# Expert blocks of one kernel listed by size class, each class in a loop of its own

## The chip, the cores and the metric

The kernel runs on one core of a Trainium2 chip. Times are device microseconds. The metric is the median of the runs of one program. A profile is one further execution of it; its times count from the start of its span.

## What is computed

A transformer layer: cross-attention on a context of 8 x 1601 keys, a self-attention block that adds zeros (its value width is 0), and a mixture of experts with the top 2 of 8 experts for each of 512 tokens. Only the last part is touched:

```python
logits = jnp.einsum('bsd,de->bse', x, router_w) + router_b
top_vals, top_idx = jax.lax.top_k(logits, top_k)
...
h = jax.nn.relu(jnp.einsum('td,edh->eth', xf, w1) + b1[:, None, :])
y = jnp.einsum('eth,ehd->etd', h, w2) + b2[:, None, :]
out = jnp.einsum('etd,te->td', y, gf)
```

x has 512 columns, the hidden layer 2048, all values are float32. Only a token's two chosen experts have a gate above zero.

## The kernel before

The program is one block of five instruction streams (TensorE, VectorE, ScalarE, GpSimd, SyncE) that wait for each other by semaphores. After attention come layer norm, router and gates, and from then on the expert stage.

**Blocks.** The tokens of an expert are worked on in blocks of up to BLOCK = 160 rows: a first part of P = 128 and a second of REST = 32. A block whose expert has at most 128 tokens left is narrow, the others are wide. VectorE works out a table from the tokens per expert (`count_sb`): for each block its expert (`table`), the first rank that it takes (`base`), and whether it is narrow (`narrow`). At the table's end stands the number of blocks. Blocks are listed in the order of the experts. Each step of this calculation waits for the one before it (`step`).

**A block.** Every float32 product is made of rounded high and low parts. For a block each of the 16 chunks c of the hidden layer goes this way: TensorE multiplies the gathered rows `xg_mix` with a piece of w1 (`hidden`, four pairs of products of 2n and n columns, where n is 128 or 160); ScalarE takes one half with the bias out of PSUM (`low_term`, writes `h_part`); VectorE adds the other (`sum_hidden`, writes `h_sum`); ScalarE applies relu and rounds (`relu_high`, writes `h_mix`); VectorE forms the low part (`relu_low`); TensorE multiplies with w2 (`outputs` in a wide block, `outputs_by_rows` with 128 rows as stationary side in a narrow one). Between these, ScalarE rounds a piece of the weights, 128x1024 (`weight_high`, `w_hi`), and VectorE forms its low part (`weight_low`, `w_lo`). TensorE runs two chunks ahead of the outputs: the products of chunks 0 and 1 of block b + 1 come at the end of block b, with 160 columns always. ScalarE's two activations on a chunk have 160 columns always, VectorE's operations have n.

**A block's end.** VectorE copies the next block's bias (`take_bias`, writes `b1_cur`; rows of the profile print `b_cur`), for which ScalarE's next `low_term` waits. In a wide block it then adds the halves of y (`sum_outputs`, writes `yt`) and TensorE turns it (`turn_outputs`); a narrow block has neither. ScalarE multiplies with the gates (`gate_rows`, writes `y_gated`), and GpSimd adds the rows to the output in memory with an indirect transfer.

**The next block's rows** are found on the way: VectorE compares ranks with `base` (`select`), TensorE turns the match into row numbers (`find_rows`), VectorE takes them (`take_rows`), GpSimd gathers the rows, TensorE turns them (`turn_rows`).

**Ahead of the loop** VectorE runs the table, copies the bias, writes the low part of `xg_mix` for block 0 (`gathered_low`) and the low part of a piece of w2, and takes the row numbers. Block 0 always belongs to expert 0, its rows are picked with a product on TensorE. TensorE makes the first two hidden products behind `xg_mix`, then runs `find_rows(0)`.

**The loops.** TensorE and VectorE have one loop over all blocks with an If in it: the code of a narrow block, then that of a wide one. ScalarE, SyncE and GpSimd have one loop and no If. SyncE loads weights two groups of four chunks ahead, whole for each block. The number of blocks and the table's entries are read from SBUF into registers (TENSOR_LOAD in the order of instructions).

```python
with pe.Fori(0, blocks) as b:
    is_narrow = pe.value_load(narrow[0:1, bass.ds(b, 1)], min_val=0, max_val=1)
    with pe.If(is_narrow > 0):
        block(b, P)
    with pe.Else():
        block(b, BLOCK)
```

## Time and profile before

| | us |
|---|---|
| median of 3 runs (1126.29 to 1127.34) | 1126.48 |
| the profiled execution | 1122.11 |
| its span | 1120.4 |
| TensorE busy in it | 1072.0 (96%) |
| VectorE busy | 976.2 (87%) |
| ScalarE busy | 732.2 (65%) |
| GpSimd busy | 504.2 (45%) |

The span runs from the first to the last instruction on the core; the profiled execution's own time has 1.7 us around it. Busy time of TensorE is that of its matmuls, which overlap, so it says that TensorE had work and not that it ran at its peak. PEclk is the granted clock of TensorE as a share of full speed (2.4 GHz; its lower level, 1.2 GHz, is 0.5). Idle time before an instruction stands in brackets with what ended it; "issue" means that the engine waited for nothing that the profile shows.

### The profile page before, as it was taken

The numbers are of one execution on the slowest core, as the hardware profiler recorded it, in microseconds if no ns is written. First come the engines' busy times: TensorE is split into PE (matmuls) and PEld (weight loads), VectorE is DVE, ScalarE is ACT, GpSimd is POOL, SyncE is SP. The second block draws the span as 40 slices with busy tenths as digits, with TensorE's granted clock in tenths as the row PEclk, the third lists the DMA queues.
The fourth block names the chain that finished last, engine by engine and source line by source line (L and its number), as shares of the span: only waits on it lengthen the run. The fifth ranks groups of instructions, "written<-read, shape, count | busy, mean of one in ns | idle before, by whom it ended". The sixth has DMA issues, their size and how long they took to land.

```text
span 1120.4 us, 24041 instructions
## 1 busy us (share of the span) xinstructions
PE 1072.0 (96%) x7583; PEld 1026.6 (92%) x7584; DVE 976.2 (87%) x2242; ACT 732.2 (65%) x1515; POOL 504.2 (45%) x448
## 2 busy tenths in 40 slices
PE   5999999999999999999999999998889999899996
PEld 5899999999999999999999999986778998789886
DVE  7589999989989999999999998988888888888985
ACT  3756665666666656666666565755578777787875
POOL 6564756566647565656475656271021121221211
PEclk9999999999999999999999999999899999999999
DMA  5322121222121212112212121044698877889883
GB/s 195 111 71 69 44 82 42 67 60 63 46 77 48 65 52 71 46 50 73 67 42 81 42 67 51 2 163 151 182 292 275 257 243 238 280 279 282 252 256 112
DMA packets 86369, 138.49 MB, mean 124 GB/s; under 512 B 15816, under 2 KB 40520, under 8 KB 86336
## 3 DMA queue, kind: packets, MB, share of 16 engines
q1 hardware_dynamic: 82800, 130.07, 36.5%
q0 software_dynamic: 3536, 8.00, 3.6%
q8 instruction: 19, 0.31, 0.1%
q14 instruction: 14, 0.11, 0.0%
HBM read 130.88 MB, written 7.17 MB: 123 GB/s over the span
## 4 chain that ended last, share of the span: by engine, by line
PE 75%; DVE 9%; ACT 8%; issue 6%; DVEq 1%; DMA 0%; POOL 0%; ACTq 0%; SPq 0%; POOLq 0%
PE ps L433 13%; PE ps L435 13%; PE ps L434 13%; PE ps L1504 8%; PE ps L1662 8%; PE ps L1554 8%; PE ps L1535 4%; PE ps L1536 4%; PE ps L1663 3%; ACT w_hi L879 2%; ACT w_hi L871 2%; DVE h_mix L1337 1%; ACT h_part L922 1%; DVE h_sum L1331 1%; DVE w_lo L1219 1%
## 5 line engine op out<-in xcount | busy, mean ns | idle before, releaser
L587 POOL TENSOR_TENSOR ctx_hi<-ctx_raw,no_query 128x1152 fp32r<-128x1152 f32 x64 | 142.2, 2221 | 259.8 <-PE ps L435 250.1
L821 ACT ACTIVATE probs<-ps,negmax 128x1152 f32<-128x1152 f32 x64 | 78.4, 1225 | 185.0 <-DVE negmax L1150 185.0
L1051 DVE SCALAR_TENSOR_TENSOR k_mix<-ps,bk_sb,k_mix 64x384 fp32r<-64x384 f32 (+1 forms) x256 | 162.3, 634 | 37.7 <-ACT k_mix L774 32.7
L433 PE MATMUL ps<-wv_hi,ctx_hi 128*128 128x256 f32 (+1 forms) x624 | 180.7, 290 | 2.2 <-DVE k_mix L1051 2.1
L591 POOL TENSOR_TENSOR ctx_lo<-ctx_raw,ctx_hi 128x1152 fp32r<-128x1152 f32 x64 | 179.8, 2809 | 5.0
L435 PE MATMUL ps<-wv_hi,ctx_lo 128*128 128x256 f32 (+1 forms) x624 | 175.0, 280 | 0.0
L434 PE MATMUL ps<-wv_lo,ctx_hi 128*128 128x256 f32 (+1 forms) x624 | 174.6, 280 | 0.0
L1662 PE MATMUL ps<-xg_mix,w_hi 128*128 128x320 f32 (+1 forms) x584 | 157.6, 342 | 14.6 <-DVE h_sum L1331 11.2
L774 ACT ACTIVATE k_mix<-ps,bk_sb 64x384 fp32r<-64x384 f32 (+1 forms) x256 | 150.9, 589 | 21.0 <-PE ps L435 16.7
L1663 PE MATMUL ps<-xg_mix,w_lo 128*128 128x160 f32 (+1 forms) x584 | 135.4, 232 | 0.0
L433 PE MATMUL ps<-ctx_hi,wk_hi 128*128 128x384 f32 (+1 forms) x384 | 133.1, 347 | 0.0
L1173 DVE TENSOR_TENSOR pt_mix<-ps,pt_mix 128x384 fp32r<-128x384 f32 (+1 forms) x256 | 132.9, 581 | 0.1
L1662 PEld LDWEIGHTS ps<-xg_mix,w_hi 128*128 128x128 f32 x584 | 112.5, 193 | 21.8 <-DVE h_sum L1331 14.9
L435 PE MATMUL ps<-ctx_hi,wk_lo 128*128 128x384 f32 (+1 forms) x384 | 132.4, 345 | 0.0
L434 PE MATMUL ps<-ctx_lo,wk_hi 128*128 128x384 f32 (+1 forms) x384 | 131.8, 343 | 0.0
L1147 DVE TENSOR_REDUCE mx<-ps 128x1 f32<-128x384 f32 (+1 forms) x256 | 128.6, 564 | 0.2 <-PE ps L1536 0.2
L779 ACT CAST v_mix<-ps 128x256 fp32r<-128x256 f32 (+1 forms) x208 | 77.4, 373 | 71.0 <-PE ps L435 69.2
L433 PEld LDWEIGHTS ps<-wv_hi,ctx_hi 128*128 128x128 f32 (+1 forms) x624 | 115.1, 184 | 4.3 <-DVE k_mix L1051 3.7
L1663 PEld LDWEIGHTS ps<-xg_mix,w_lo 128*128 128x128 f32 x584 | 114.1, 195 | 2.8
L434 PEld LDWEIGHTS ps<-wv_lo,ctx_hi 128*128 128x128 f32 (+1 forms) x624 | 115.3, 185 | 0.3
L435 PEld LDWEIGHTS ps<-wv_hi,ctx_lo 128*128 128x128 f32 (+1 forms) x624 | 114.9, 184 | 0.0
L832 ACT CAST pt_mix<-ps 128x384 fp32r<-128x384 f32 (+1 forms) x256 | 111.5, 530 | 0.2 <-PE ps L1554 0.2
(236 smaller groups left out, 2606.4 us busy)
## 6 DMA issues: line engine op xcount, KB each, us to landing
w_raw<-in_w_dram SPq DMA_DIRECT2D x76, 1024.0 KB, 6.9
ctx_raw<-in_ctx_t_dram SPq DMA_DIRECT2D x48, 576.0 KB, 3.8
ctx_raw<-in_ctx_t_dram SPq DMA_DIRECT2D x16, 673.5 KB, 4.1
out_dram<-acc POOLq DMA_DIRECT2D x2, 1024.0 KB, 10.2
q_both<-q_scratch SPq DMA_DIRECT2D x14, 128.0 KB, 2.9
x<-in_x_dram SPq DMA_DIRECT2D x4, 256.0 KB, 3.6
wq_raw<-in_wq_dram SPq DMA_DIRECT2D x1, 1024.0 KB, 6.8
q_scratch<-q_out SPq DMA_DIRECT2D x1, 1024.0 KB, 7.0
```

The costliest lines, as they stand in the source:

```text
L433: pe.matmul(acc_ap, a_hi, b_hi, start=start, stop=False)
L434: pe.matmul(acc_ap, a_hi, b_lo, start=False, stop=False)
L435: return pe.matmul(acc_ap, a_lo, b_hi, start=False, stop=stop)
L587: nc.gpsimd.tensor_tensor(ctx_hi[slot][:, :, 0:n], ctx_raw[slot][:, :, 0:n], no_query[:].rearrange("p (o i) -> p o i", o=1).broadcast_to([ ...
L591: nc.gpsimd.tensor_tensor(ctx_lo[slot][:, :, 0:n], ctx_raw[slot][:, :, 0:n], ctx_hi[slot][:, :, 0:n].bitcast(F32), ALU.subtract).then_inc( ...
L774: last = nc.scalar.activation(k_mix[rows, 2 * a + i, KEY0[c]:KEY0[c] + m], ps[rows, bank, 0:m], ACT.Identity, bias=bk_sb[rows, a:a + 1])
L832: nc.scalar.copy(pt_mix[:, TILE0[c]:TILE0[c] + n, 0, :], ps[:, SCORE_BANK + c, 0:n * P].rearrange("p (t r) -> p t r", t=n)).then_inc(pt_hi ...
L1051: last = nc.vector.scalar_tensor_tensor(out=k_mix[other, 2 * a + i, cols], in0=ps[rows, bank, 0:m], scalar=bk_sb[rows, a:a + 1], in1=k_mix ...
L1147: part = nc.vector.tensor_reduce(mx[:, c:c + 1], ps[:, SCORE_BANK + c, 0:KEYS[c]], AX.X, ALU.max)
L1173: nc.vector.tensor_tensor(pt_mix[:, TILE0[c]:TILE0[c] + m, 1, :], ps[:, SCORE_BANK + c, 0:m * P].rearrange("p (t r) -> p t r", t=m), pt_mi ...
L1662: pe.matmul(both, hi, mix[:, :, 0:n], start=first, stop=False)
L1663: return pe.matmul(high, lo, mix[:, 0, 0:n], start=False, stop=end)
```

## The change

The blocks are put in order of size: first block 0, which is expert 0's first 160 tokens and counts as wide whatever expert 0 holds, then the other wide blocks, then the narrow ones. `count_sb` of expert 0 is lowered by 160 for the list. A key of 16 times the size class plus the block's number is compared with all keys (`past`, now 16x16), which gives each block its place, and from it `table` and `base` in the new order. The table ends in three numbers (where the wide ones end, where a class of larger blocks would end, which this size doesn't have, and the number of blocks), and each engine reads all three. The table of flags, `narrow`, is gone. TensorE, VectorE and ScalarE have a loop over wide blocks and, if there are narrow ones, a second loop over these. In narrow blocks ScalarE's two activations have 128 columns, and so have the products of the next block's chunks 0 and 1, if this one is narrow. SyncE and GpSimd keep their one loop. GpSimd fills two more small constants, next to those that it filled before. `yt`, `past` and `past_n` move to other places in SBUF. The calculation of the table on VectorE stands as rows behind the diff.

```diff
     BLOCK = P + REST
+    WIDE = P + P // 4
...
-    MAX_BLOCKS = (TOP_K * T + (E - 1) * (BLOCK - 1)) // BLOCK + 1
+    MAX_BLOCKS = (TOP_K * T + E * (BLOCK - 1)) // BLOCK + 1
     TABLE = MAX_BLOCKS + 1
+    GROUP = 16
+    ENDS = 3
+    assert 2 * BLOCK <= 480 and TABLE <= GROUP
...
+        def ends_loaded(engine):
+
+            return [engine.value_load(table[0:1, TABLE + i:TABLE + i + 1], min_val=1, max_val=MAX_BLOCKS)
+                    for i in range(ENDS)]
...
-            act.wait_ge(table_ready, 1)
-            blocks = act.value_load(table[0:1, TABLE:TABLE + 1], min_val=1, max_val=MAX_BLOCKS)
-            def low_term(b, c):
+            def low_term(b, c, n):
...
-                nc.scalar.activation(h_part[:, c % 2, :], ps[:, hidden_bank(c), BLOCK:2 * BLOCK], ACT.Identity,
+                nc.scalar.activation(h_part[:, c % 2, 0:n], ps[:, hidden_bank(c), BLOCK:BLOCK + n], ACT.Identity,
                                      bias=b1_cur[:, 0, c:c + 1]).then_inc(h_parted, 1)
...
                 take_bias_product(2 * c + 1)
-                relu_high(0, c)
-            with act.Fori(0, blocks) as b:
+            def block_high(b, n, ahead):
...
                 for c in range(HIDDEN_AHEAD, HT):
-                    low_term(b, c)
+                    low_term(b, c, n)
...
+            act.wait_ge(table_ready, 1)
+            wide_end, large_end, blocks = ends_loaded(act)
+            with act.Fori(0, wide_end) as b:
+                block_high(b, WIDE, BLOCK)
+            with act.If(blocks > wide_end):
+                with act.Fori(wide_end, blocks) as b:
+                    block_high(b, P, P)
...
-            select(0, rank_e[:, 0:1, :], 0.0, gates_e[:, 0, :, :])
+            select(0, rank_e[:, 0:1, :], 0.0, gates_e[:, 0, :, :], most=float(WIDE))
...
+            step(nc.vector.tensor_scalar(count_sb[:, 0:1], count_sb[:, 0:1], float(WIDE), 0.0, ALU.subtract, ALU.max))
             step(nc.vector.tensor_scalar(some[:], count, 0.0, None, ALU.is_gt))
-            step(nc.vector.memset(some[:, 0:1], 1.0))
...
+            step(nc.vector.scalar_tensor_tensor(out=left[:], in0=order[:], scalar=float(GROUP), in1=block_no[:],
+                                                op0=ALU.mult, op1=ALU.add))
+            keys = left[:]
+            step(nc.vector.tensor_tensor(past[:], by_other(keys).broadcast_to(blocks_wide),
+                                         by_block(keys).broadcast_to(blocks_wide), ALU.is_le))
...
+            step(nc.vector.tensor_tensor(ends, by_other(keys).broadcast_to([P, ENDS, TABLE]),
+                                         by_block(limits[:]).broadcast_to([P, ENDS, TABLE]), ALU.is_lt))
+            step(nc.vector.tensor_reduce(start2[:, 0:ENDS], ends, AX.X, ALU.add))
+            step(nc.vector.tensor_scalar(table_f[:, TABLE:TABLE + ENDS], start2[:, 0:ENDS], 1.0, None, ALU.add))
...
-            blocks = dve.value_load(table[0:1, TABLE:TABLE + 1], min_val=1, max_val=MAX_BLOCKS)
...
+            wide_end, large_end, blocks = ends_loaded(dve)
+
+            def block_low(b, n):
+                expert_next = dve.value_load(table[0:1, bass.ds(b + 1, 1)], min_val=0, max_val=E - 1)
                 for c in range(HT):
...
                 take_bias(bass.ds(expert_next, 1))
-                if n == BLOCK:
-                    sum_outputs(b)
+                if n > P:
+                    sum_outputs(b, n)
                 else:
                     dve.sem_inc(y_summed, KD)
-            dve.wait_ge(narrow_ready, 1)
-            with dve.Fori(0, blocks) as b:
-                expert_next = dve.value_load(table[0:1, bass.ds(b + 1, 1)], min_val=0, max_val=E - 1)
-                is_narrow = dve.value_load(narrow[0:1, bass.ds(b, 1)], min_val=0, max_val=1)
-                with dve.If(is_narrow > 0):
-                    block_low(b, expert_next, P)
-                with dve.Else():
-                    block_low(b, expert_next, BLOCK)
+            with dve.Fori(0, wide_end) as b:
+                block_low(b, WIDE)
+            with dve.If(blocks > wide_end):
+                with dve.Fori(wide_end, blocks) as b:
+                    block_low(b, P)
             for c in range(HIDDEN_AHEAD):
-                sum_hidden(blocks, c)
+                sum_hidden(blocks, c, P)
...
-                    if n == BLOCK:
-                        outputs(b, c)
+                    if n > P:
+                        outputs(b, c, n)
                     else:
                         outputs_by_rows(b, c)
-                hidden(b + 1, 0)
-                if n == BLOCK:
-                    turn_outputs(b)
+                hidden(b + 1, 0, ahead)
+                if n > P:
+                    turn_outputs(b, n)
                 else:
                     pe.wait_ge(y_product, KD * (b + 1))
                     pe.sem_inc(y_turned, BT)
-                hidden(b + 1, 1)
-
-            with pe.Fori(0, blocks) as b:
-                is_narrow = pe.value_load(narrow[0:1, bass.ds(b, 1)], min_val=0, max_val=1)
-                with pe.If(is_narrow > 0):
-                    block(b, P)
-                with pe.Else():
-                    block(b, BLOCK)
+                hidden(b + 1, 1, ahead)
+
+            with pe.Fori(0, wide_end) as b:
+                block(b, WIDE, BLOCK)
+            with pe.If(blocks > wide_end):
+                with pe.Fori(wide_end, blocks) as b:
+                    block(b, P, P)
```

VectorE, the table: from the count to the low part of `xg_mix`. First the kernel before, the middle left out:

```order
L1366 COPY count_sb<-ps 128x8 [waits counts_product]
L1368 TENSOR_SCALAR some<-count_sb 128x8 [waits vector_step]
...
L1380 TENSOR_TENSOR past<-sums3,block_no 128x120 [waits vector_step]
L1381 TENSOR_TENSOR past_n<-past,sums0 128x120 [waits vector_step]
L1382 TENSOR_REDUCE owner<-past 128x15
L1383 TENSOR_SCALAR table_f<-owner 128x15 [waits vector_step]
L1384 COPY table_f<-sums3 128x1
L1385 CAST table<-table_f 128x16 [waits vector_step]
L1386 TENSOR_REDUCE start<-past_n 128x15
...
L1396 TENSOR_SCALAR narrow<-left2 128x15 [waits vector_step]
L1326 COPY b1_cur<-b1_sb 128x16
L1319 TENSOR_TENSOR xg_mix<-ps,xg_mix 128x2x160 [waits xg_high] x2
```

And the kernel changed, its second half (the names as before; `order` is a block's class and then its place, `left` the keys):

```order
L1432 TENSOR_TENSOR past<-left 128x256 [waits vector_step]
L1434 TENSOR_REDUCE order<-past 128x16 [waits vector_step]
L1435 TENSOR_TENSOR past<-order,block_no 128x256 [waits vector_step]
L1437 TENSOR_TENSOR past_n<-past,owner_held 128x256 [waits vector_step]
L1438 TENSOR_REDUCE table_f<-past_n 128x16 [waits vector_step]
L1440 TENSOR_TENSOR past_n<-left,limits 128x48 [waits vector_step]
L1442 TENSOR_REDUCE start2<-past_n 128x3 [waits vector_step]
L1443 TENSOR_SCALAR table_f<-start2 128x3 [waits vector_step]
L1444 CAST table<-table_f 128x19 [waits vector_step]
L1445 TENSOR_TENSOR past_n<-past,base_unordered 128x256
L1446 TENSOR_REDUCE base<-past_n 128x16 [waits vector_step]
L1350 COPY b1_cur<-b1_sb 128x16 [waits vector_step]
```

The bias copy followed `narrow`, the last of the operations on tiles of up to 120 elements. Now a second half of operations on 256 and 48 elements stands ahead of it, and the copy waits for `base`; `table`, which the other engines wait for, is written near the end instead of midway.

VectorE at the loop's entry, before (the reads of `table` and `narrow`, then the first operation on block 0):

```order
L1403 TENSOR_LOAD table [waits table_ready]
L1403 ISA x2
L1429 UNCONDITIONAL_BRANCH [waits narrow_ready]
L1429 ISA
L1430 TENSOR_LOAD table
L1430 ISA x2
L1431 ISA
L1431 TENSOR_LOAD narrow
L1431 ISA x2
L1432 COMPARE_AND_BRANCH
L1330 ISA
L1331 TENSOR_TENSOR h_sum<-ps,h_part 128x128 [waits h_parted]
```

And changed:

```order
L441 TENSOR_LOAD table [waits table_ready]
L441 ISA x2
L441 TENSOR_LOAD table
L441 ISA x2
L441 TENSOR_LOAD table
L441 ISA x2
L1479 UNCONDITIONAL_BRANCH
L1479 ISA
L1457 TENSOR_LOAD table
L1457 ISA x2
L1354 ISA
L1355 TENSOR_TENSOR h_sum<-ps,h_part 128x160 [waits h_parted]
```

The flag's read and the compare are gone, two reads of the table's ends are new, and the first h_sum has 160 columns instead of 128.

ScalarE at the same place, in the kernel changed (before, the only read stood ahead of its first copy of xg_mix, and nothing stood between h_mix and the loop's branch):

```order
L941 ACTIVATE h_mix<-h_sum 128x160 [waits h_summed]
L441 TENSOR_LOAD table [waits table_ready]
L441 ISA x2
L441 TENSOR_LOAD table
L441 ISA x2
L441 TENSOR_LOAD table
L441 ISA x2
L995 UNCONDITIONAL_BRANCH
L995 ISA
L935 ACTIVATE h_part<-ps,b1_cur 128x160 [waits h_ready]
```

Three reads now lie between the relu of chunk 1 and the low term of chunk 2.

## Rows read from the trace of the kernel before

**Rows 1.** Busy time by stretch; the marks are b_cur and first h_sum.

```profile
core 0: us, PE busy (x) PEld busy (x) DVE busy (x) ACT busy (x) POOL busy (x), PEclk, DMA share, GB/s
796.29:828.13 31.84, 30.67 (x189) 27.52 (x189) 28.43 (x65) 24.46 (x49) 4.01 (x3) 0.89 0.96 297
828.13:829.83 1.70, 0.65 (x6) 0.46 (x4) 0.17 (x2) 1.33 (x2) 0.00 (x0) 1.00 0.59 34
829.83:862.49 32.66, 29.45 (x189) 26.18 (x189) 28.69 (x65) 25.42 (x50) 5.68 (x4) 0.95 0.86 274
...
864.04:899.23 35.19, 34.54 (x259) 34.15 (x259) 29.88 (x65) 25.82 (x51) 5.89 (x4) 0.95 0.85 258
899.23:901.35 2.12, 1.98 (x14) 1.37 (x13) 1.76 (x7) 1.18 (x2) 0.00 (x0) 1.00 0.47 16
901.35:935.66 34.31, 34.31 (x272) 33.83 (x269) 29.78 (x65) 25.93 (x51) 5.90 (x4) 1.00 0.80 263
935.66:937.62 1.96, 1.82 (x12) 1.25 (x11) 1.76 (x7) 1.02 (x2) 0.00 (x0) 1.00 0.00 0
...
968.75:970.13 1.38, 0.66 (x6) 0.47 (x4) 0.17 (x2) 1.10 (x2) 0.00 (x0) 1.00 0.27 10
970.13:1001.27 31.14, 28.46 (x189) 25.04 (x189) 28.51 (x64) 25.49 (x51) 5.69 (x4) 1.00 0.91 290
1001.27:1002.84 1.57, 0.66 (x6) 0.47 (x4) 0.17 (x3) 1.29 (x2) 0.00 (x0) 1.00 0.54 21
...
1106.96:1120.40 13.44, 3.43 (x24) 2.62 (x22) 2.31 (x8) 4.22 (x8) 2.97 (x2) 0.81 0.20 24
```

**Rows 2.** VectorE in order of time, the table (start us, us, instruction).

```profile
785.24 0.17 DVE L1366 COPY count_sb<-ps 128x8 f32<-128x8 f32 x1
...
786.37 0.57 DVE L1375 TENSOR_TENSOR sums<-sums 128x8 f32<-128x8 f32 x3
786.98 0.28 DVE L1380 TENSOR_TENSOR past<-sums,block_no 128x120 f32<-128x120 f32 x1
787.29 0.28 DVE L1381 TENSOR_TENSOR past_n<-past,sums 128x120 f32<-128x120 f32 x1
787.49 0.27 DVE L1382 TENSOR_REDUCE owner<-past 128x15 f32<-128x120 f32 x1
787.80 0.17 DVE L1383 TENSOR_SCALAR table_f<-owner 128x15 f32<-128x15 f32 x1
787.88 0.14 DVE L1384 COPY table_f<-sums 128x1 f32<-128x1 f32 x1
...
790.11 0.17 DVE L1326 COPY b_cur<-b_sb 128x16 f32<-128x16 f32 x1
```

**Rows 3.** In order of time: entry into the loop, and after block 0.

```profile
790.81 0.39 PE L1662 MATMUL ps<-xg_mix,w_hi 128*128 128x320 f32 x1 [0.16 <-DVE xg_mix L1319]
...
796.29 0.29 DVE L1331 TENSOR_TENSOR h_sum<-ps,h_part 128x128 f32<-128x128 f32 x1 [2.34 <-issue]
...
796.63 0.19 PEld L1662 LDWEIGHTS ps<-xg_mix,w_hi 128*128 128x128 f32 x1 [3.15 <-DVE h_sum L1331]
...
832.00 0.58 PE L1662 MATMUL ps<-xg_mix,w_hi 128*128 128x256 f32 x1 [3.22 <-issue]
```

**Rows 4.** Stretches inside block 0, columns as in rows 1.

```profile
798.00:800.00 2.00, 1.68 (x5) 1.41 (x6) 1.92 (x5) 2.00 (x5) 1.22 (x1) 0.50 0.02 6
...
803.00:806.00 3.00, 3.00 (x18) 2.86 (x18) 2.90 (x11) 1.50 (x3) 0.00 (x0) 0.74 1.07 227
```

**Rows 5.** Groups by form from 640 us: the exponential on ScalarE.

```profile
L821 ACT ACTIVATE probs<-ps,negmax 128x1152 f32<-128x1152 f32 x12 | 14.7, 1225 | 34.4 <-DVE negmax L1150 34.4
...
L824 ACT ACTIVATE probs<-ps,negmax 128x449 f32<-128x449 f32 x12 | 7.5, 629 | 0.0
```

**Rows 6.** ScalarE in order of time, inside block 0.

```profile
820.24 0.34 ACT L928 ACTIVATE h_mix<-h_sum 128x160 fp32r<-128x160 f32 x1 [0.16 <-DVE h_sum L1331]
```

**Rows 7.** DMA queues from 820 to 840 us: packets, MB, share.

```profile
q8 instruction: 2, 0.03, 0.6%
```

More of the change, by code:

```diff
@@ new lines, in _ @@
+            step(nc.vector.tensor_reduce(left[:], is_past_n, AX.X, ALU.add))
+            nc.vector.scalar_tensor_tensor(out=base_unordered[:], in0=start2[:], scalar=float(BLOCK), in1=left2[:],
+                                           op0=ALU.mult, op1=ALU.add)
+            step(nc.vector.scalar_tensor_tensor(out=start[:], in0=start2[:], scalar=float(-BLOCK), in1=left[:],
+                                                op0=ALU.mult, op1=ALU.add))
+            step(nc.vector.scalar_tensor_tensor(out=order[:], in0=start[:], scalar=0.0, in1=two_more[:],
+                                                op0=ALU.is_le, op1=ALU.add))
@@ new lines, in _ @@
+            nc.vector.tensor_scalar(left[:], start[:], float(P), -2.0, ALU.is_gt, ALU.mult)
+            step(nc.vector.scalar_tensor_tensor(out=left2[:], in0=start[:], scalar=float(2 * T), in1=order[:],
+                                                op0=ALU.is_gt, op1=ALU.add))
+            step(nc.vector.tensor_tensor(order[:], left2[:], left[:], ALU.add))
+            step(nc.vector.scalar_tensor_tensor(out=left[:], in0=order[:], scalar=float(GROUP), in1=block_no[:],
+                                                op0=ALU.mult, op1=ALU.add))
```

126 lines of the change are left out of this document (69 added, 57 removed).

## The prediction

> **What bounds the kernel now.** I read the page's shares first, then the expert stage in stretches, then single stretches in order of time. The program is limited by TensorE nearly everywhere, and the change touches nothing ahead of 785 us, so only the expert stage has to be priced. A block's mark on VectorE is the copy of its bias (b_cur); the next block's work starts there with the first h_sum. Between these marks the stage falls into nine bodies and eight boundaries [rows 1]. A narrow body lasts 31.14 us, and neither engine fills it: TensorE 28.46, VectorE 28.51. A wide body at full clock lasts 34.31 us and TensorE is busy in all of it. Boundaries: wide to wide 2.12 us, wide to narrow 1.96, narrow to narrow 1.38, narrow to wide 1.57. By these lengths, the trace runs narrow, narrow, wide, wide, narrow, narrow, wide, narrow, wide. That is what the inputs give: working through the reference's router, the experts get 97, 74, 148, 154, 127, 62, 214 and 148 tokens, and expert 6 needs two blocks (160 and 54).
>
> Three places depart from the regular lengths. The first block's body takes 31.84 us with the clock at 0.89, and block 1's takes 32.66 us at 0.95 [rows 1]. Two of the wide bodies, both after a narrow block, have the clock at 0.95 and take 35.19 and 35.17 us (the first of them is in [rows 1]), so a short stretch at the lower level costs a wide body 0.88 us.
>
> **The new list of blocks.** Block 0 is now wide by its code, whatever expert 0 holds. Expert 0 has 97 tokens, so nothing of it is left for the list. Listed wide are experts 2, 3, 6 and 7, then narrow 1, 4, 5 and the rest of 6. So the count stays nine, but there are five wide and four narrow blocks where there were four and five. The program has no size beyond 160 that could take expert 6 in one block. One narrow block has become a wide one: 34.31 - 31.14 = 3.2 us, ahead of any effect of the clock.
>
> **The table on VectorE.** Before, the work from the count to the bias copy runs from 785.24 to 790.11, 4.87 us [rows 2]. Its unit prices: a small operation that the next one waits for takes 0.20 us from start to start, one of 120 elements 0.31, one that nobody waits for 0.08 (small) or 0.20 (120 elements). 105 more elements cost 0.28 - 0.17 = 0.11 us, so one of 256 elements takes 0.42 and a step of it 0.45. After: 16 small steps 3.3, five small ones that nobody waits for 0.4, six steps of 128 elements 1.9, one unwaited 0.2, two on the three ends 0.5, seven of 256 elements 3.15. Together 9.45 us, **4.6 more**. Nothing hides it: TensorE's first hidden product waits for xg_mix, which VectorE writes right behind the bias copy [rows 3]. ScalarE no longer waits for the table ahead of its xg_mix, but VectorE's half comes after the table anyway, so that is worth nothing.
>
> **Entry into the loop.** VectorE stands 2.34 us before its first h_sum, and TensorE 3.15 us for it [rows 3]. In that time VectorE reads three numbers from the table and takes two branches; now it reads four and takes one. I take a third of the stall, 0.7 us, for a read and nothing for a branch: **+0.7**, bounds 0 and 1.2. ScalarE gets three reads between its second relu and the third chunk, where it had none. At the same rate that is 2.1 us, but a wide body leaves ScalarE eight us idle (25.93 busy of 34.31), and TensorE is two chunks behind. I take 0; the bound is 1.5.
>
> **The clock ahead of block 0.** TensorE will stand 4.6 us longer ahead of its first hidden product. It runs at the upper level there now. The 3 us stall at the loop's entry is followed by a stretch at the lower level, from 798 to about 804.5 [rows 4]; the stall after block 0 is followed by another (0.95 in that body). So I expect the two products and the search for rows, 2.7 us at full clock, to run partly at half: **+1.5**, bounds 0 and 2.5, since VectorE's take_rows waits for them.
>
> **Block 0's body.** It now is wide and falls into the same slow stretch. A narrow body with some 6.5 us at half clock lost 31.84 - 31.14 = 0.7 us, because TensorE had room. A wide one has none: a stretch of about half that length cost 0.88, and a further 3.3 us at half cost up to 1.6 more. 34.31 + 2.4 - 31.84 = **+4.9**; bounds 34.31 + 0.9 - 31.84 = 3.4 and 34.31 + 3.4 - 31.84 = 5.9.
>
> **Everything from block 0's bias copy to the last one.** Before: 828.13 to 1106.96, 278.83 us. After: four boundaries wide to wide 8.48, four wide bodies 137.24, one wide to narrow 1.96, four narrow bodies 124.56, three narrow to narrow 4.14: 276.4. In it are three gains: the stall after block 0 goes (TensorE resumes at 832.00, though h_sum, begun at 829.83 and 0.29 us long, was there at 830.12 [rows 1, 3]), and so do two slow stretches in wide bodies; the dearer wide boundaries give back 1.1. On top, in narrow blocks ScalarE's two activations per chunk shrink from 160 to 128 columns. From 449 to 1152 columns the exponential grows from 629 to 1225 ns [rows 5], 0.85 ns a column, so 27 ns each. In the steady part VectorE and ScalarE wait for each other once in two chunks, and ScalarE stands 0.16 us for h_sum there [rows 6]: the ring has two such activations, 0.054 us a pair of chunks, 0.43 a block, 1.7 in four. TensorE's narrower first two chunks lie beside other work: 0. If-branches inside the loop lie under waits of 1.38 to 2.12 us: 0. So 274.7, **-4.2**; bounds -5 (wide to narrow without cost, more from ScalarE) and -2 (two us for the first entry into the narrow loop's code).
>
> A page bears on that entry. The Trainium skill, Runtime: NRT & Kernel Launch, section Instruction fetch mechanics, says that only two pages of code are held and that a taken branch to elsewhere waits for its page to be fetched. The stall after block 0 is such a case, with two instruction packets in those 20 us [rows 7]; but the 1.38 us boundary has the same jumps over the wide code and back, and no stall.
>
> **The end.** The last block is narrow now. A wide block's end has the sums and turns of y; 2.12 - 1.57 = 0.55 us less of it: **-0.5**. The 13.44 us behind the last bias copy [rows 1] otherwise stay, since they are the last rows' scatter.
>
> **Sum.** 4.6 + 0.7 + 1.5 + 4.9 - 4.2 - 0.5 = +7.0 us. On the profiled execution's 1122.11 us that is 1129.1. The median of the runs shown is 1126.48, 4.4 us above it; I add the same difference: **1133.5 us**, slower by 0.6%.
>
> **Rivals.**
> - *The slow stretch falls into the longer gap.* TensorE stands some five us up to 795.4, and the clock may be back when block 0 begins. Then the 1.5 and the 2.4 go: +3.1, 1129.6 us. Against: each of the stalls of 3 us had its slow stretch behind it, not inside. 22%.
> - *New stalls.* The narrow loop's first entry or first jump back costs the 2 us seen after block 0, and ScalarE's three reads reach VectorE (1.5): +10.5, 1137 us. For: rows 3 show such a stall once. 15%.
> - *Not slower: the narrow body closes its gaps.* VectorE is busy in 28.51 of 31.14 us. If ScalarE is what keeps it waiting everywhere, and not just in the ring above, four narrow bodies give up to 4 x 2.63 = 10.5 instead of 1.7. The sum is then -1.8, 1124.7 us. It decides from a narrow body of 29.4 us down. Against: TensorE itself is busy for 28.5 us there, and part of VectorE's idle time is at the block's last chunk, where it waits for a cast of unchanged size. 8%; with the first rival on top it would be faster by 5 us.
> - *Every jump back pays.* By the page named above, a loop whose body exceeds what is held would stall at each jump back. As a mechanism here: seven jumps of 1.9 us, +20 us in all, 1146 us. Against: the attention loop's body of 616 TensorE instructions jumps back without an idle stretch, as do the later blocks. 4%.
> - *The list isn't what I worked out.* If block 0's expert had over 128 tokens, nothing would be added; the first body's length, narrow, speaks against it. 3%.
>
> **How the numbers follow.** The forecast itself has 45%, the small remainder lies between the cases. The range reaches from below the first rival to a little above the second: 1127.5 to 1139 us. 0.2% is 2.25 us, about what a measurement of this kernel can tell from no change. Slower by more: forecast, new stalls, every jump, and most of the first rival, 78%. Within: 14%. Faster: 8%.
>
> **What would show it.** In the changed kernel's profile: h_sum with 160 columns 80 times in the loop and 128 columns 64 times; 9.4 us from count_sb to b_cur; the first hidden product at about 795.4; first h_sum of block 0 near 803; four wide bodies of 34.3 without a slow stretch; narrow bodies of 30.7; the last bias copy near 1114. I am wrong if the table takes less than 8 us, if block 0's body takes 34.5 or less, or if a narrow body leaves the span 30.2 to 31.2.

## The result, and the profile after

The changed kernel takes 1129.50 us (median of 11 runs, 1126.11 to 1131.48), the kernel before in the same comparison 1126.09 (11 runs, 1122.61 to 1127.34). The ratio is 1.0033, 95% interval 1.0020 to 1.0046: slower by 3.7 us, from 2.3 to 5.2. That ratio isn't the quotient of the two medians, which lie 3.4 us apart; differences given "by the ratios" below are such ratios times the time of the kernel before. The forecast was +7.0 us and 1133.5 us. The direction came out, the size was about double.

The profiled execution of the changed kernel took 1130.01 us, with a span of 1128.2. First the expert stage in stretches, with the same marks as rows 1. The columns are the stretch, its length, the busy time of TensorE, its weight loads, VectorE, ScalarE and GpSimd with their counts, then PEclk (the granted clock of TensorE as a share of full speed), the busy share of the DMA engines and GB/s.

```profile
797.29:805.75 8.46, 4.63 (x24) 4.57 (x24) 3.58 (x10) 1.46 (x3) 0.00 (x0) 0.70 0.50 182
805.75:841.68 35.93, 35.55 (x259) 35.34 (x260) 29.88 (x65) 24.79 (x49) 4.22 (x3) 0.91 0.87 260
841.68:843.35 1.67, 1.59 (x11) 1.07 (x9) 1.67 (x6) 0.74 (x2) 0.00 (x0) 1.00 0.49 18
843.35:877.87 34.52, 34.45 (x273) 34.06 (x272) 29.86 (x65) 26.36 (x51) 5.94 (x4) 1.00 0.83 261
...
986.45:988.12 1.67, 1.58 (x11) 1.07 (x9) 1.67 (x6) 0.74 (x2) 0.00 (x0) 1.00 0.05 13
988.12:1019.21 31.09, 29.58 (x204) 26.38 (x204) 28.60 (x65) 25.37 (x51) 5.71 (x4) 1.00 0.88 291
1019.21:1019.89 0.68, 0.41 (x4) 0.26 (x3) 0.17 (x2) 0.40 (x2) 0.00 (x0) 1.00 0.06 24
1019.89:1051.18 31.29, 28.19 (x190) 24.96 (x191) 28.62 (x64) 25.48 (x51) 5.63 (x4) 1.00 0.89 284
...
1051.86:1083.50 31.64, 29.49 (x190) 26.23 (x191) 28.58 (x65) 25.55 (x51) 5.63 (x4) 0.95 0.90 287
...
1115.48:1128.20 12.72, 0.40 (x4) 0.26 (x3) 0.75 (x4) 4.04 (x8) 2.97 (x2) 0.66 0.22 26
```

Five wide bodies come first, then four narrow ones, as worked out. Block 0's body lasts 35.93 us with the clock at 0.91; the other four wide ones last 34.50 to 34.54 us at full clock. There is no stall behind block 0: 1.67 us and then a regular body, where rows 1 and 3 had 1.70 and a further stand of TensorE up to 832.00. Nor is there one at the first entry into the narrow loop (1.67 us at 986.45, then 31.09).

The table on VectorE in order of time (start us, us, instruction), to be read against rows 2:

```profile
787.81 0.17 DVE L1390 COPY count_sb<-ps 128x8 f32<-128x8 f32 x1
...
792.91 0.17 DVE L1428 TENSOR_TENSOR order<-left 128x16 f32<-128x16 f32 x1
793.12 0.17 DVE L1429 SCALAR_TENSOR_TENSOR left<-order,block_no 128x16 f32<-128x16 f32 x1
793.33 0.42 DVE L1432 TENSOR_TENSOR past<-left 128x256 f32<-128x256 f32 x1
793.79 0.42 DVE L1434 TENSOR_REDUCE order<-past 128x16 f32<-128x256 f32 x1
...
797.29 0.17 DVE L1350 COPY b_cur<-b_sb 128x16 f32<-128x16 f32 x1
```

787.81 to 797.29 is 9.48 us, against 4.87. A small step starts 0.21 us after the last, one of 256 elements takes 0.42 us and 0.46 to the next.

The entry into the loop, in order of time, against rows 3:

```profile
798.01 0.61 PE L1710 MATMUL ps<-xg_mix,w_hi 128*128 128x320 f32 x1 [6.47 <-DVE xg_mix L1343]
...
802.67 0.16 DVE L1326 CAST idx_next<-ps 128x1 uint32<-128x1 f32 x1 [2.15 <-PE ps L1690]
...
805.75 0.33 DVE L1355 TENSOR_TENSOR h_sum<-ps,h_part 128x160 f32<-128x160 f32 x1 [2.73 <-issue]
...
806.13 0.63 PE L1710 MATMUL ps<-xg_mix,w_hi 128*128 128x320 f32 x1 [3.49 <-DVE h_sum L1355]
...
809.73 0.40 ACT L935 ACTIVATE h_part<-ps,b_cur 128x160 f32<-128x160 f32 x1 [1.69 <-issue]
```

And the clock there, columns as above:

```profile
795.60:802.00 6.40, 3.99 (x17) 4.02 (x18) 4.74 (x11) 1.46 (x3) 0.00 (x0) 0.50 0.07 10
802.00:806.00 4.00, 0.63 (x9) 0.55 (x8) 0.60 (x6) 0.00 (x0) 0.00 (x0) 0.93 1.02 393
806.00:809.00 3.00, 2.87 (x12) 2.87 (x13) 3.00 (x6) 1.92 (x5) 0.73 (x1) 0.50 0.41 153
```

TensorE stands 6.47 us for the table, and its granted clock is at the lower level (0.50, 1.2 GHz) while it makes the two hidden products ahead of the loop. VectorE therefore waits 2.15 us for the row numbers. The clock is back in the next idle stretch, falls again toward the end of the 3.49 us stall, and block 0's work on TensorE starts at the lower level.

The stage, from count_sb to the end of the span, term by term:

| us | before | after | measured | forecast |
|---|---|---|---|---|
| count_sb to b_cur (table) | 4.87 | 9.48 | +4.61 | +4.6 |
| b_cur to first h_sum (entry, clock) | 6.18 | 8.46 | +2.28 | +2.2 |
| block 0's body | 31.84 | 35.93 | +4.09 | +4.9 |
| its bias copy to the last one | 278.83 | 273.80 | -5.03 | -4.2 |
| the last bias copy to the end | 13.44 | 12.72 | -0.72 | -0.5 |
| sum | 335.16 | 340.39 | +5.23 | +7.0 |

In these two executions count_sb comes at 785.24 and at 787.81. The change touches hardly anything ahead of it, and in the nine profiles taken below the mark falls between 784.71 and 787.28, in kernels of both kinds. So those 2.57 us are put down to the execution, not to the change, and the stage is compared from count_sb.

### The profile page after: what moved, and what is told of

The parts are those of the page before. It is cut to its first block, busy times and chain, and to the rows that moved or that the text cites. A ratio compares the mean times of both kernels' runs of the same rounds, so it can differ in the third digit from the quotient of the medians.

```text
span 1128.2 us, 24178 instructions
## 1 busy us (share of the span) xinstructions
PE 1075.7 (95%) x7671; PEld 1033.8 (92%) x7671; DVE 983.8 (87%) x2260; ACT 729.5 (65%) x1515; POOL 504.2 (45%) x450
## 4 chain that ended last, share of the span: by engine, by line
PE 76%; DVE 9%; ACT 8%; issue 5%; DMA 1%; DVEq 1%; POOL 0%; SPq 0%; ACTq 0%; POOLq 0%
PE ps L446 13%; PE ps L448 13%; PE ps L447 13%; PE ps L1710 9%; PE ps L1552 8%; PE ps L1602 8%; PE ps L1583 4%; PE ps L1584 4%; PE ps L1711 4%; ACT w_hi L895 2%; ACT w_hi L887 1%; DVE h_mix L1361 1%; DVE w_lo L1242 1%; DVE w_lo L1250 1%; DVE h_sum L1355 1%
```

## The experiments

All times of one row below are against runs of the kernel before on the same chip. "Stage" is count_sb to the end of the span in the profiled execution.

| kernel | median us (runs) | ratio to before, interval | stage |
|---|---|---|---|
| before, first profile | 1126.09 (11) | | 335.16 |
| before, once more | 1123.79 (1) | | 335.77 |
| after | 1129.50 (11) | 1.0033, 1.0020 to 1.0046 | 340.39 |
| before, block 0 wide | 1126.35 (12) | 1.0017, 1.0005 to 1.0030 | 339.22 |
| before, table 15 steps longer | 1132.09 (6) | 1.0063, 1.0050 to 1.0077 | 342.37 |
| after, half of the table as constants | 1121.05 (7) | 0.9969, 0.9957 to 0.9981 | 334.39 |
| after, narrow blocks first | 1123.44 (12) | 0.9985, 0.9976 to 0.9994 | 334.90 |
| after, bias copy early | 1124.06 (12) | 0.9988, 0.9978 to 0.9997 | 335.36 |
| after, two reads for three | 1128.61 (12) | 1.0026, 1.0015 to 1.0037 | 339.82 |
| narrow first, bias early, two reads | 1119.66 (6) | 0.9949, 0.9935 to 0.9962 | 333.40 |
| the same, output bias early too | 1121.16 (4) | 0.9956, 0.9940 to 0.9973 | 332.19 |

**Before once more** gives the spread of one profile.

> The kernel before, unchanged, for a second profile. The stage behind the count took 335.16 us in the first. The changed kernel's took 5.2 us more, but the times say 3.7, so I expect a stage of about 336 to 337 us here, with more slow stretches in wide bodies behind narrow ones (0.9 us each; there were two in three); if it is within 0.3 of 335.16 the difference lies ahead of the count, where the two profiles differ by 2.6 us.

The stage took 335.77 us, 0.6 more than in the first profile and less than the 336 to 337 expected; the table took 4.86 and the entry 6.17, as there. The stall behind block 0 is longer here, though:

```profile
834.75 0.57 PE L1662 MATMUL ps<-xg_mix,w_hi 128*128 128x256 f32 x1 [4.95 <-issue]
```

and block 1's body is 35.06 us, while no wide body has a slow stretch, where more of them had been expected. So single bodies move by 2.4 us between executions of one kernel. Against this profile the changed kernel's stage is 4.6 us longer.

**Block 0 wide** in the kernel before, nothing else:

```diff
             step(nc.vector.tensor_tensor(left2[:], left[:], base[:], ALU.subtract))
+            step(nc.vector.memset(left2[:, 0:1], float(BLOCK)))
```

> The kernel before, with one part of the change alone: block 0 is marked as wide, so that five blocks are wide and four narrow, in the old order and with the old loops and table. My theory (the loss is the sum of a longer table, 4.6 us, a longer entry into the loop, 2.3, and a wide block 0, 4.1, less about 5.7 given back later): +3.5 to +4.5 us on the kernel before, block 0's body near 36 us instead of 31.8, the table unchanged but for one step of 0.1 us. Rival (the width of block 0 costs nothing by itself, the loss is the table): within 1 us of the kernel before.

The entry and block 0 with the body behind it:

```profile
795.37 0.16 DVE L1302 CAST idx_next<-ps 128x1 uint32<-128x1 f32 x1 [1.87 <-PE ps L1643]
...
798.52 0.33 DVE L1331 TENSOR_TENSOR h_sum<-ps,h_part 128x160 f32<-128x160 f32 x1 [2.81 <-issue]
```

```profile
798.52:834.52 36.00, 35.51 (x259) 35.30 (x260) 29.77 (x65) 24.77 (x49) 4.22 (x3) 0.91 0.82 245
834.52:836.47 1.95, 1.79 (x12) 1.22 (x11) 1.75 (x7) 1.02 (x2) 0.00 (x0) 1.00 0.23 25
836.47:867.61 31.14, 29.65 (x202) 26.32 (x201) 28.55 (x64) 25.55 (x51) 5.68 (x4) 1.00 0.89 289
```

The body is 36.00 us, as in the changed kernel (35.93), at the same clock. The narrow body behind it is regular, 31.14 us, so the stall after block 0 goes with the width of block 0 already, without the new loops. The stage is 3.5 to 4.1 us longer than in the two profiles of before; the timed runs give +1.9 us by the ratio (0.6 to 3.4), with medians only 0.7 us apart, where 3.5 to 4.5 were expected. So what a wide block 0 costs is shown by the profile, and by the narrow-first run below; this run's times alone don't part it from the rival's 1 us. 2.06 us of the stage's difference lie in the entry, where I had expected at most the stall: VectorE waits 1.87 us for the row numbers here, too, although the table is hardly longer (5.00 us). That has to do with where the clock falls, which is taken up below.

**A longer table** in the kernel before: 15 waited operations of 120 elements, whose result nobody reads.

```diff
+            for _ in range(15):
+                step(nc.vector.tensor_tensor(past_n[:], past[:], past[:], ALU.mult))
             take_bias(slice(0, 1))
```

> The kernel before, with 15 more operations of 120 elements, each waited for, ahead of the bias copy on VectorE: 15 x 0.31 = 4.65 us, what the new table adds. Nothing else is changed. My theory: +4.6 us for the operations and 1.5 us for TensorE's first hidden products at the lower clock behind the longer gap, so +5 to +6.5 us; the first h_sum comes 11.8 to 12.5 us behind the end of the old chain's start instead of 6.2. Rival (the longer gap is absorbed, since the clock is back when block 0 begins): +3 us or less.

```profile
791.79 4.71 DVE L1398 TENSOR_TENSOR past_n<-past 128x120 f32<-128x120 f32 x15
...
802.33 0.16 DVE L1302 CAST idx_next<-ps 128x1 uint32<-128x1 f32 x1 [2.55 <-PE ps L1644]
```

+7.1 us (5.6 to 8.7) for 4.7 us of table, a little more than the 5 to 6.5 expected. The rest is the entry, 8.46 us for 6.18: the products ahead of the loop run at the lower level here too, and VectorE waits 2.55 us for the row numbers instead of 0.28. The longer table alone gives the changed kernel's entry; no new loop or list is needed for it. Nor is a longer table for most of it: with block 0 wide the entry was 8.24 us behind a table of 5.00.

**Half of the table as constants** in the changed kernel. GpSimd writes the list, the three ends and the bases for these inputs in its idle time, and the calculation from `order` on is left out (the kernel then holds for these inputs only).

```diff
+            nc.gpsimd.memset(table_f[:, 1:2], 2.0).then_inc(rows_cleared, 1)
...
-            step(nc.vector.scalar_tensor_tensor(out=order[:], in0=start[:], scalar=0.0, in1=two_more[:],
-                                                op0=ALU.is_le, op1=ALU.add))
...
-            step(nc.vector.tensor_reduce(base[:], past_n[:], AX.X, ALU.add))
```

> The changed kernel, without the second half of the table on VectorE: the order of the blocks, their first ranks and the three ends are written as constants by GpSimd beforehand, with the values that they have for these inputs. From the count to the bias copy that leaves about 4.8 us instead of 9.5. My theory: 4.6 us less for the table, and 1.5 to 2 less since the first hidden products run at the upper clock again: 5 to 6.5 us under the changed kernel, 1 to 3 us under the kernel before. Rival (the loss sits in block 0 and the loops, the table is hidden): within 1 us of the changed kernel.

The table takes 4.69 us and the time is 3.5 us under the kernel before (2.1 to 4.8), 7.2 us by the ratios under the changed one, where 1 to 3 and 5 to 6.5 were expected. So with a table of the old length the new order and loops are a gain. It and the longer table agree in the timed runs: these 4.7 to 4.8 us cost 7.1 to 7.2 with what follows from them. The mechanism named beforehand came out only in part. The first hidden products don't run at the upper clock throughout, the entry is 7.35 us (8.46 in the changed kernel, 6.18 before), and VectorE waits 1.04 us for the row numbers:

```profile
789.50:794.00 4.50, 3.52 (x24) 3.47 (x24) 3.46 (x9) 1.46 (x3) 0.00 (x0) 0.76 0.00 0
```

```profile
793.66 0.16 DVE L1343 CAST idx_next<-ps 128x1 uint32<-128x1 f32 x1 [1.04 <-PE ps L1684]
```

**Narrow blocks first** in the changed kernel: block 0 takes 128 rows (97 tokens), the loop over narrow blocks stands first, the wide one second.

```diff
-    WIDE = P + P // 4
+    WIDE = P
...
-            with pe.Fori(0, wide_end) as b:
+            with pe.Fori(0, large_end) as b:
                 block(b, WIDE, BLOCK)
-            with pe.If(blocks > wide_end):
-                with pe.Fori(wide_end, blocks) as b:
-                    block(b, P, P)
+            with pe.If(blocks > large_end):
+                with pe.Fori(large_end, blocks) as b:
+                    block(b, BLOCK, BLOCK)
```

(VectorE and ScalarE likewise; the size class counts the other way.)

> The changed kernel with the classes the other way round: block 0 is expert 0's first 128 rows and runs in the loop of narrow blocks, which comes first; the wide ones follow. Four wide and five narrow blocks again, the table as long as in the changed kernel, first reads and branches the same. The narrow loop's look-ahead has 160 columns again. My theory: 4 us under the changed kernel (block 0's body 31.5 to 32 us instead of 35.9), 0.7 us back for the wide end, a slow stretch or two: 2.5 to 4 us under the changed kernel, so within 1.5 us of the kernel before. Rival (block 0 in the slow stretch costs the same whatever its class): within 1 us of the changed kernel.

1.7 us under the kernel before (0.7 to 2.7), 5.4 by the ratios under the changed one. Block 0's body is 31.33 us for 35.93, and the bodies behind it are as in the changed kernel (31.29 to 31.39 narrow, 34.52 to 34.75 wide). The changed kernel's stage is 5.5 us longer. 4.6 of that is block 0, since the slow stretch at the entry costs the narrow body nearly nothing; 1.6 lies behind it, where five boundaries of 0.71 and three of 1.67 us stand for three of 0.68 and five of 1.67; the wide end takes 0.7 back. The expectation (2.5 to 4) had allowed less for block 0 and nothing for the boundaries.

**The bias copy early** in the changed kernel: the copy of the bias and the low part of xg_mix stand in the middle of the table.

```diff
             step(nc.vector.tensor_reduce(left[:], is_past_n, AX.X, ALU.add))
+            take_bias(slice(0, 1))
+            gathered_low(0)
...
-            take_bias(slice(0, 1))
-            gathered_low(0)
```

> The changed kernel with VectorE's bias copy and low part of xg_mix moved from the end of the table to its middle (ahead of the operation on base_unordered); nothing is left out. TensorE's first two hidden products and the search for rows then run beside the table's second half, so the 2.15 us for which VectorE stood behind them go. My theory: from the count to the first h_sum 15.8 us instead of 17.9, so 2 us less than the changed kernel, unless TensorE's longer stand right ahead of block 0 gives block 0 a longer slow stretch (up to 1.5 us back). Rival (VectorE's chain alone sets the entry, the lower clock of the first products is no part of the loss): no difference.

1.3 us under the kernel before (0.3 to 2.5), 5 under the changed one, where two were expected. In order of time:

```profile
790.55 0.39 PE L1710 MATMUL ps<-xg_mix,w_hi 128*128 128x320 f32 x1 [1.29 <-DVE xg_mix L1343]
...
798.96 0.32 DVE L1355 TENSOR_TENSOR h_sum<-ps,h_part 128x160 f32<-128x160 f32 x1 [0.47 <-issue]
...
799.34 0.64 PE L1710 MATMUL ps<-xg_mix,w_hi 128*128 128x320 f32 x1 [6.01 <-DVE h_sum L1355]
```

TensorE makes its first products at full clock during the rest of the table, so VectorE finds the row numbers ready. From count_sb to the first h_sum it is 13.42 us, against 17.94. The surprise is VectorE's stand ahead of the loop: 0.47 us for 2.73, with the same four reads and the same branch. The price is paid elsewhere: TensorE then stands 6.01 us, and block 0's body is 36.17 us.

**Two reads for three.** Of the three ends TensorE, VectorE and ScalarE read two, SyncE and GpSimd one.

```diff
-            return [engine.value_load(table[0:1, TABLE + i:TABLE + i + 1], min_val=1, max_val=MAX_BLOCKS)
-                    for i in range(ENDS)]
+            first, last = [engine.value_load(table[0:1, TABLE + i:TABLE + i + 1], min_val=1, max_val=MAX_BLOCKS)
+                           for i in (0, 2)]
+            return first, first, last
```

> The changed kernel, with two of the table's three ends read by TensorE, VectorE and ScalarE (the one that nothing uses is left out) and one by SyncE and GpSimd. If a read costs about 0.4 to 0.7 us, VectorE's idle time ahead of its first h_sum falls from 2.73 to 2.0 to 2.4 us and ScalarE's ahead of chunk 2 from 1.69 to about 1.1; my theory: 0.3 to 0.7 us less in all, hardly to be told by the times, but by the trace. Rival: the idle time ahead of the loop is one for its branch and new code, and does not move.

```profile
805.00 0.33 DVE L1356 TENSOR_TENSOR h_sum<-ps,h_part 128x160 f32<-128x160 f32 x1 [2.13 <-issue]
```

The stand is 0.60 us shorter (2.13 for 2.73), the price of a read on VectorE there, near the 0.7 taken in the forecast. The time is 0.8 us under the changed kernel's by the ratios (1.0026 and 1.0033), with intervals that overlap, so the times don't tell it from nothing.

**All three together**, with ScalarE's two reads moved ahead of its first activation on a chunk, where it stood idle for the table:

```diff
             gathered_high(0)
+            act.wait_ge(table_ready, 1)
+            wide_end, large_end, blocks = ends_loaded(act)
```

> Narrow blocks first (as in e4), with the bias copy and xg_mix in the middle of the table (as in e5), two ends read instead of three (as in e6), and ScalarE's reads ahead of its first copy of the outputs' bias. It leaves nothing out. If the parts add up: 2.1 + 0.4 us under e4, which was 1.7 us under the kernel before, so about 4 us under the kernel before and 8 us under the changed kernel. Rival (a longer slow stretch in block 0 eats what the entry gains): as e4, 1.5 to 2 us under the kernel before.

5.7 us under the kernel before (4.3 to 7.3), where about 4 were expected; this beats both kernels. It isn't yet regular: block 0's body is 35.07 us for a narrow block. VectorE stands in it:

```profile
816.54 0.17 DVE L1338 COPY idx_cur<-idx_next 128x2 uint32<-128x2 uint32 x1 [2.78 <-DMA out_dram<-acc]
```

**The output bias early too.** ScalarE copies the output's bias (acc) ahead of the loop's first activations, so that GpSimd's transfer of it starts at 793.36 instead of 800.60. Its reads of the table's ends move back behind its first two low terms.

```diff
             gathered_high(0)
-            act.wait_ge(table_ready, 1)
-            wide_end, large_end, blocks = ends_loaded(act)
             act.wait_ge(rows_moved, 16)
+            for t in range(2 * HIDDEN_AHEAD):
+                take_bias_product(t)
             act.wait_ge(b1_set, 1)
+            low_term(0, 0, WIDE)
+            low_term(0, 1, WIDE)
+            act.wait_ge(table_ready, 1)
+            wide_end, large_end, blocks = ends_loaded(act)
             for c in range(HIDDEN_AHEAD):
-                take_bias_product(2 * c)
-                low_term(0, c, WIDE)
-                take_bias_product(2 * c + 1)
                 relu_high(0, c, WIDE)
```

> The version with narrow blocks first, bias and low part ahead of the second half of the table, and two reads; now also with ScalarE's four copies of the output bias (acc) right behind its half of xg_mix, where it stood idle for 8.5 us, so that the transfer of acc to the output starts some 8 us earlier. If the 2.78 us for which VectorE's copy of the row numbers (idx_cur) waited in block 0 there is for that transfer's landing, the wait goes, block 0's body is back from 35.07 to about 31.3 us and the time falls by about 3 us, to some 0.7 to 0.8% under the kernel before. If the long body came from the slow stretch and the wait only hid in it, or if another transfer then takes its place, the body stays above 33.5 us and the time within 1 us of that version.

The wait is gone and block 0's body is 31.14 us, as the first theory had it. But the time isn't lower, where about 3 us less were expected: the ratio is 0.9956, and 0.9949 for the version ahead of it, from only 4 and 6 runs and with overlapping intervals. By the profiles, of the 3.9 us that block 0's body gains, 1.8 are given back at the entry and 0.9 behind block 0; the stage is 1.2 us shorter.

```profile
801.40 0.29 DVE L1357 TENSOR_TENSOR h_sum<-ps,h_part 128x128 f32<-128x128 f32 x1 [1.72 <-issue]
```

In the version ahead of it this h_sum started at 798.19 with no idle time listed.

## Why the prediction was right, and where it was off

By number the result, 1129.50 us, is that of the first rival (1129.6) and not of the forecast (1133.5); the range holds both. What tells them apart is the profile, term by term.

**The table** was priced at +4.6 us and measured +4.61. The unit prices of rows 2 carried over, and the figure for 256 elements, drawn out from 15 and 120, was right to 0.01 us. That nothing hides it is shown twice, by the longer table in the kernel before (+7.1 us) and by the constants in the changed one.

**Entry and clock**, +2.2 forecast, +2.28 measured. The read cost 0.4 of VectorE's stand (2.73 for 2.34), or 0.6 in the experiment; the clock's part is VectorE's wait for the row numbers, 2.15 us for 0.28. The first rival (the slow stretch falls into the longer gap) is out for this place: some 2.4 us of that stretch did fall into the gap, but the clock was still at 0.50 while TensorE made its products. That this term came out to 0.1 us is in part luck. The forecast put the 1.5 down to the longer gap, but with block 0 wide VectorE waited 1.87 us behind a table of 5.00, and with half of the table as constants 1.04 behind one of 4.69. So what the gap itself adds to that wait isn't parted from where the clock fell ahead of it, which is taken up at the end of this section.

**Block 0's body**, +4.9 forecast, +4.09 measured; its bounds were 3.4 to 5.9. The step was the slow stretch's price in a wide body, 2.4 us over 34.31: it is 1.6 (35.93), 1.7 in the kernel before with a wide block 0, and 1.9 with the bias early. Against the changed kernel's own wide bodies (34.52) the 1.6 is 1.4. Giving the further half-clock stretch its full loss was too much. ScalarE's reads do show: 1.69 us of "issue" at 809.73, for which VectorE waits 1.12 us. That is the 1.5 that I had left at 0, but TensorE, two chunks ahead and slow, was busy nearly throughout: 35.55 us of 35.93. In the version with two reads this body is 0.5 us shorter (35.43), but with half of the table as constants and all three reads it is 35.38, so no run shows that the reads cost it anything.

**The rest of the stage**, -4.2 forecast, -5.03 measured. Here two terms were wrong in opposite directions. I had said that the If-branches lie under waits and cost 0. A boundary between narrow blocks, before:

```profile
969.03 0.39 ACT L922 ACTIVATE h_part<-ps,b_cur 128x160 f32<-128x160 f32 x1 [1.46 <-DVE b_cur L1326]
...
970.13 0.29 DVE L1331 TENSOR_TENSOR h_sum<-ps,h_part 128x128 f32<-128x128 f32 x1 [1.22 <-ACT h_part L922]
```

and after:

```profile
1019.50 0.37 ACT L935 ACTIVATE h_part<-ps,b_cur 128x128 f32<-128x128 f32 x1 [1.46 <-DVE b_cur L1350]
...
1019.89 0.29 DVE L1355 TENSOR_TENSOR h_sum<-ps,h_part 128x128 f32<-128x128 f32 x1 [0.52 <-ACT h_part L935]
1020.83 1.23 DVE L1242 TENSOR_TENSOR w_lo<-w_raw,w_hi 128x1024 fp32r<-128x1024 f32 x1 [0.64 <-ACT w_hi L887]
```

Before, h_part ended at 969.42 and h_sum began at 970.13, 0.71 us later, although the row names ScalarE as the releaser. So something else came last there; VectorE's own reads and branches are what stands between the two. Now h_sum follows h_part by 0.02 us, and the boundary is 0.68 us for 1.38 (wide to wide 1.67 for 2.12). But what follows waits for ScalarE's weight piece in both: w_lo begins 1.64 us after the bias copy before (970.39) and 1.62 after. So this gain of 0.70 us is only moved into the body, and the narrow bodies are 31.3 us and not the 30.7 forecast. Over body and boundary together a narrow block takes 31.29 + 0.68 = 31.97 us against 31.14 + 1.38 = 32.52: -0.55, where the forecast by ScalarE's narrower activations was -0.43. The size fits, but that the activations are its cause isn't shown: a wide block and its boundary take 34.52 + 1.67 = 36.19 us against 36.43, so -0.24 without any narrower activation, and the narrow block may have as much from there. I had 0 for that; four of them are 0.95 us, and this term was short by 0.9. A sum per interval between bias copies would have been safe from this.

Of the two items that carried this term one is borne out: the stall behind block 0 goes. The other came out too, in that no wide body behind block 0 has a slow stretch (one narrow body has, 31.64 us at 0.95), but the second profile of the kernel before has none in its wide bodies either. So the 1.8 us for it belong to one execution and not surely to the change; the longer stall of that second profile hid this in the sum. With the bias copy, the end gave -0.72 for -0.5.

**Other rivals.** New stalls: none at the narrow loop's first entry, or at any jump back. That the narrow body closes its gaps to 29.4 us: no, 31.3. That one was named as a sign of being wrong (a narrow body outside 30.2 to 31.2 us), and by it the split of the narrow block was: the bodies take 31.09, 31.29, 31.64 and 31.30. That the list is another: no, five wide bodies and four narrow ones. Every jump back pays: no, boundaries got shorter. (The forecast's 616 TensorE instructions for a pass of the attention loop aren't borne out by the counts, which give about 640 matmuls and as many weight loads; TensorE is busy 100.00 us of 100 there, so the argument stands.) This also bears on the page cited in the forecast (Trainium skill, Runtime: NRT & Kernel Launch, Instruction fetch mechanics): by its rule each jump back over a long body would wait for its code. The eight boundaries, seven of them with a jump back, take 0.68 to 1.67 us and show no such wait here, while a stall as it describes stood in both profiles of the kernel before just behind block 0, once, and not where block 0 was wide.

**From +7.0 to the timed +3.7.** The profiles account for 1.8 of it: -0.8 in block 0, -0.8 in the rest, -0.2 at the end, against +0.1 ahead of the loop. The remaining 1.5 us, from +5.2 in the first pair of profiles to +3.7 in the timed runs (which reach to 5.2), has a likely cause that I missed in the profile of before. Three fences with columns as above: the first 3 us from count_sb on in the first profile of the kernel before, the same in the second, and the same with block 0 wide, there with the stretch of the first hidden products under it:

```profile
785.24:788.24 3.00, 3.00 (x16) 3.00 (x15) 2.56 (x16) 0.45 (x1) 0.00 (x0) 0.62 0.00 0
```

```profile
786.23:789.23 3.00, 3.00 (x15) 3.00 (x15) 2.56 (x16) 0.45 (x1) 0.00 (x0) 0.60 0.00 0
```

```profile
785.28:788.28 3.00, 3.00 (x23) 2.96 (x22) 2.56 (x16) 0.46 (x1) 0.00 (x0) 1.00 0.00 0
791.00:795.00 4.00, 4.00 (x20) 4.00 (x20) 2.50 (x3) 0.98 (x3) 0.00 (x0) 0.57 0.74 237
```

In both profiles of before the clock is at its lower level for part of this stretch, while VectorE is at the table. TensorE's work in front of the loop lasts longer for it, it stands only 0.16 us for xg_mix [rows 3], and the products behind run at full clock. In the profile with block 0 wide, and in seven of the eight other kernels' (all but the last experiment's), the clock is full here; TensorE is done earlier, stands longer for the table (1.98 us at 790.98), and is slow behind that. An execution of the kernel before that goes the second way would lose some 1.6 us at its entry (an estimate, 1.87 - 0.28), and the profiles would then overstate what the change costs by as much. Both profiles of it went the first way, and no profile shows the other. Two more figures bear on it. The profiled executions of the kernel before took 1122.11 and 1123.79 us, under every median of its timed runs (1125.15 to 1126.48). And against the first profile the stage differences of seven of the eight experiments lie 1.4 to 4.0 us above what the times give, as the changed kernel's does by 1.5. In the eighth, the longer table, profile and times agree (+7.2 and +7.1), which this cause doesn't explain. So it stays likely and open. It was to be seen beforehand: the forecast took the full clock at 790.81 as the state of that place, without looking at what had run ahead of it.

## What to carry to other kernels

A calculation that every engine waits for costs its length, and it can cost more behind it by what happens to TensorE's clock: here 4.7 us of table took 7.1 in the timed runs. Before pricing such a step, look at the clock ahead of the place as well as at it. What the first work behind it doesn't need should stand behind that work's inputs, and the block that falls into the slow stretch should be the one with room in it. Price a loop from mark to mark over a whole turn, since time taken out of a boundary often comes back as a wait a microsecond later.

## What the runs showed of the hardware

**Reads into registers.** The stand of VectorE ahead of its loop was 2.32 to 2.34 us with three reads and two branches, 2.73 with four reads, 2.13 with three and one branch, but 0.47 with four in the version with the bias early, and no idle time was listed in the combined one. With three reads and block 0 wide in the kernel before it was 2.81, so the number of reads alone doesn't set it. Two things differ in the short ones: the work ahead of the reads had long been able to run, and the DMA engines were idle. In the last version, where the output's bias was on its way, the stand was 1.72. The stretches ahead of the first h_sum, first of the combined version, then of the last one:

```profile
796.30:798.20 1.90, 0.00 (x0) 0.00 (x0) 1.90 (x7) 1.31 (x3) 0.00 (x0) 0.50 0.00 0
```

```profile
799.70:801.40 1.70, 0.00 (x0) 0.00 (x0) 0.00 (x0) 0.00 (x0) 0.00 (x0) 0.50 1.12 206
```

DMA share 0.00 in the one and 1.12 in the other; it is 1.04 in the changed kernel's stand of 2.73 us, and in that of the kernel before. That busy DMA engines make the reads or the fetching of code slower fits all of these, but no run varied it alone, so it is left as likely and not shown.

**Code not yet run.** The kernel before stood 3.2 to 5.0 us once, behind its first narrow block, where TensorE has to pass wide code that hadn't run yet. With a wide first block it was gone, and VectorE's stand at the loop's entry, where it now has to pass the narrow code, was 2.81 us for 2.34. With narrow blocks first in a loop of their own, where no wide code has to be passed, there is no such stall either: 0.71 us, then a body of 31.33. In the 2.8 us of VectorE's stand with block 0 wide one instruction packet landed, and none in the stands of the kernel before and of the changed one. The cause by code loading is argued from this, not shown.

**The clock.** At the table and the entry it fell to its lower level behind, or late in, stands of TensorE of 1.67 us (half of the table as constants) and more, and in three profiles between 784 and 786 us, behind a stand of 1.01 us for VectorE. The profile with block 0 wide has that stand, too, and the clock stays full there. What the stretch inside block 0 costs goes by the room that TensorE has: 0.7 us in the kernel before's narrow body (31.84 for 31.14), nothing that shows with narrow blocks first (31.33, as the bodies behind it), 1.1 to 1.9 in a wide one (35.38 to 36.17 for 34.31).
